# Graph-transformer layer with an LSTM: row stages in chunks of 256 rows, one ahead of the loop and four inside it

## The reference

```python
# layer 0, graph branch (agg: attention-weighted sums per node)
att = agg.reshape(n, C) @ Wo.T + bo
x = x + att
z = _layernorm(x, ln_ff_g, ln_ff_b)
h = jax.nn.silu(z @ W1.T + b1)
ff = h @ W2.T + b2
return x + ff
# layer 0, recurrent branch, on _layernorm(x), 1250 time steps
combined = jnp.concatenate((x_t, h_prev), axis=1)
f_t = jax.nn.sigmoid(combined @ W_f + b_f)
i_t = jax.nn.sigmoid(combined @ W_i + b_i)
c_tilde = jnp.tanh(combined @ W_c + b_c)
c_t = f_t * c_prev + i_t * c_tilde
o_t = jax.nn.sigmoid(combined @ W_o + b_o)
h_t = o_t * jnp.tanh(c_t)
```

## Time and profile before

| what | us |
|---|---|
| runs | 7319.33, 7336.98, 7514.56 |
| median | 7336.98 |
| the profiled execution | 7332.33 |
| its span, first to last instruction | 7330.6 |
| mean granted TensorE clock in it | 0.927 of full |

### The profile page before, as it was taken

How to read it: one execution, slowest core, us unless ns; L and a number is a source line. 1 busy time by engine, 2 the same in 40 slices (tenths; PEclk the granted TensorE clock), 3 DMA queues, 4 the chain that set the end, 5 groups by cost and what they waited for, 6 DMA issues and landing times. The chain is left out here.

```text
span 7330.6 us, 411790 instructions
## 1 busy us (share of the span) xinstructions
PE 5252.2 (72%) x180989; PEld 3541.9 (48%) x180989; DVE 3870.4 (53%) x22246; ACT 1844.6 (25%) x8790; POOL 875.2 (12%) x891
## 2 busy tenths in 40 slices
PE   1256354775977777777777777777777777877799
PEld 1122122442555555555555555555555555553445
DVE  6115355733466666666666666666666666573112
ACT  1001004820033333333333333333333333200011
POOL 0717563500000000000000000000000000350000
PEclk7677677987999999999999999999999999997899
DMA  2116465511000000000000000000000000230100
GB/s 71 40 70 200 138 175 100 159 37 46 0 0 0 0 0 0 0 0 0 0 0 0 0 0 0 0 0 0 0 0 0 0 0 0 86 80 23 46 0 15
DMA packets 116203, 235.83 MB, mean 32 GB/s; under 512 B 65390, under 2 KB 67054, under 8 KB 112251
## 3 DMA queue, kind: packets, MB, share of 16 engines
q0 software_dynamic: 56032, 162.48, 7.9%
q1 hardware_dynamic: 60058, 72.02, 3.2%
HBM read 219.99 MB, written 14.45 MB: 32 GB/s over the span
## 5 line engine op out<-in xcount | busy, mean ns | idle before, releaser
L1422 PE MATMUL l_bank<-l_w,l_hp 128*32 128x128 f16 x160000 | 2464.4, 219 | 998.7 <-DVE l_hp L1531 993.6
L1422 PEld LDWEIGHTS l_bank<-l_w,l_hp 128*32 128x32 f16 x160000 | 2246.3, 97 | 1633.0 <-DVE l_hp L1531 1627.4
L1495 DVE STREAM_TRANSPOSE l_turn<-l_bank 128x128 f32<-128x128 f32 x2500 | 794.5, 318 | 1180.0 <-PE l_bank L1422 1005.6
L1461 ACT ACTIVATE l_th<-l_z 128x8 f32<-128x8 f32 x2500 | 523.3, 209 | 2127.1 <-DVE l_z L1501 2127.1
L1443 PE MATMUL l_spare<-l_w 128*2 128x512 f16 x15000 | 1025.7, 379 | 0.0
L1674 POOL DMA_INDIRECT ga_rows<-r_table,dst_t x176 | 168.0, 955 | 4643.7 <-DMA r_table<-c_r 4516.4
L1466 ACT ACTIVATE l_tc<-l_th 128x2 f32<-128x2 f32 x2500 | 490.9, 196 | 464.3 <-DVE l_th L1518 464.3
L1507 DVE SCALAR_TENSOR_TENSOR l_terms<-l_th 128x4 f32<-128x4 f32 x2500 | 359.2, 144 | 256.1 <-ACT l_th L1461 256.1
L1525 DVE TENSOR_TENSOR l_hp<-l_go,l_tc 128x2 f16<-128x2 f32 x2500 | 422.0, 169 | 130.4
L1501 DVE TENSOR_REDUCE l_z<-l_turn 128x8 f32<-128x24 f32 x2500 | 447.2, 179 | 42.6
L1531 DVE TENSOR_TENSOR l_hp<-l_full,l_hp 128x2 f16<-128x2 f32 x2500 | 422.2, 169 | 43.2
(11 more groups left out here) (413 smaller groups left out, 4896.0 us busy)
## 6 DMA issues: line engine op xcount, KB each, us to landing
keys<-in_src_by_tile SPq DMA_DIRECT2D x7, 1344.0 KB
e_w<-in_e_W SPq DMA_DIRECT2D x2, 4096.0 KB
w<-in_g_W SPq DMA_DIRECT2D x2, 2048.0 KB, 10.4
l_wh<-in_l_Wh SPq DMA_DIRECT2D x1, 4096.0 KB
l_wx<-in_l_Wx SPq DMA_DIRECT2D x1, 4096.0 KB
e_w<-in_e_W SPq DMA_DIRECT2D x2, 2048.0 KB
sm_q_rows<-q_table,sorted_e POOLq DMA_INDIRECT x176
sm_k_rows<-k_table,sorted_e POOLq DMA_INDIRECT x176
```

The costliest lines, as they stand in the source:

```text
L1422: mm = pe.matmul(banks[par][q][32 * j:32 * j + 32, 0:128], hp[:, par, k, 30 - 30 * v:62 - 30 * v], w16[:, part, k, j, 256 * q + 128 * v:25 ...
L1461: act.activation(th[:, 2 * q:2 * q + 2, 1:], z[:, q, :].rearrange("p (j m) -> p j m", m=GATES), ACT.Tanh, scale=2.0 ** -Z_BITS).then_inc(s ...
L1495: dve.transpose(turn[:, par, q, :, 1:33], banks[par][q][:, 0:128].rearrange("p (m r) -> p m r", r=32)).then_inc(s_turned[q], 1)
```

## The change

The stages from the denominators to the input projection are no longer run over all rows. Rows are cut into five chunks of W = 256. The work on one chunk is a list of 101 numbered pieces, and each engine has at most one of its own per number:

| pieces | work | TensorE, per piece |
|---|---|---|
| 0 to 3 | transposes, copy on ScalarE | two transposes |
| 4 to 11 | output product, residual on VectorE | two matmuls of 256 columns |
| 12 to 24 | feed-forward LayerNorm | two matmuls in four pieces |
| 25 to 40 | first product; tanh form of silu on ScalarE | two matmuls |
| 41 to 56 | second product | two matmuls |
| 57 to 68 | LayerNorm for the recurrence | two matmuls in four pieces |
| 69 to 100 | input projection, written by ScalarE | two matmuls |

Chunk 0 runs ahead of the loop, all pieces one after another, with the packing of Wh and the remaining divisions between them. Chunks 1 to 4 run inside the loop: chunk c has its piece i at the end of step 256(c - 1) + i, on each engine behind that engine's own part of the step. These steps are written out (416 in all, with the few at chunk borders); the others stay in hardware loops, now five. A step in which TensorE has a piece issues four spare matmuls in place of twelve. The sigmoid becomes 0.5 (1 + tanh(x/2)), so ScalarE needs no table but that of tanh, except for the root: there it loads the table of the root and afterwards that of tanh again. `xp` holds two chunks instead of all rows and is scratch for the chunk being made. W2 and Wo share a buffer, and SyncE reloads them for each chunk. The maximum of Wh and its scales move into `scatter_and_tables`, with a 4 MB read of Wh ahead of the other weights there; Wh (again), Wo, W1 and the small columns load during `attend`; Wx loads into Wh's place after the packing.

The diff, cut to its core:

```diff
 def scatter_and_tables(...):
         def _(pool):
 ...
+            pool.wait_ge(topped, 1)
+            pool.partition_all_reduce(top[:, 1:2], top[:, 0:1], P, RMAX).then_inc(reduced, 1)
             pool.wait_ge(scattered, 16 * ET)
         def _(sp):
             for k in range(KC):
                 sp.dma_start(x[:, k, :], d["x"][:, k * NP:(k + 1) * NP]).then_inc(x_in, 16)
+            sp.dma_start(wh[:, :], d["l_Wh"]).then_inc(wh_in, 16)
             for dst, src in loads:
 ...
         def _(dve):
             for layer, (src, dst) in enumerate(((x, xn), (xn, z))):
+                if layer == 1:
+                    dve.wait_ge(wh_in, 16)
+                    g.link(dve, dve.tensor_reduce(top[:, 0:1], wh[:, :], AX.X, ALU.max, apply_absolute_value=True))
+                    dve.tensor_scalar(top[:, 0:1], top[:, 0:1], 2.0 ** -20, None, ALU.max).then_inc(topped, 1)
 def attend(...):
+        def _(sp):
+            for dst, src in loads:
+                sp.dma_start(dst, src).then_inc(loaded, 16)
+            sp.wait_ge(loaded, 16 * len(loads))
 ...
+W = 256
+CHUNKS = RT * P // W
+TURN, WO, LNF, FF1, FF2, LNL, XIN, STEPS = 0, 4, 12, 25, 41, 57, 69, 101
 ...
         def _(sp):
+            for c in range(CHUNKS):
+                wait_pe(sp, c, LNF - 1)
+                sp.dma_start(wo_w2, d["g_W2"]).then_inc(w2_in, 16)
+                if c == 0:
+                    sp.wait_ge(s_packed, M16)
+                    sp.dma_start(late[:, :], d["l_Wx"]).then_inc(wx_in, 16)
+                if c < CHUNKS - 1:
+                    wait_pe(sp, c, LNL - 1)
+                    sp.dma_start(wo_w2[:, 0:KC * C], d["g_Wo"]).then_inc(wo_in, 16)
 ...
         def _(pe):
+            def step(t, par, c=0, i=None):
 ...
-                for k in range(3):
+                busy = i is not None and on_pe(i)
+                for k in range(1 if busy else 3):
                     for j in range(4):
                         pe.matmul(spare[32 * j:32 * j + 2, 0:512], w16[:, 0, k, j, 0:2], w16[:, 0, k, j, :],
                                   start=True, stop=True)
-            with pe.Fori(0, N, 2) as t:
+                if busy:
+                    rows_step(c, i)
+            for i in range(STEPS):
+                if on_pe(i):
+                    rows_step(0, i)
+            pe.wait_ge(s_packed, M16)
+            for c in range(1, CHUNKS):
+                a = (c - 1) * W
+                for t in range(a - 2 if a else 0, a):
+                    step(t, t % 2)
+                for i in range(STEPS + 1):
+                    step(a + i, i % 2, c, i if i < STEPS else None)
+                with pe.Fori(a + STEPS + 1, a + W - 2, 2) as t:
+                    step(t, 0)
+                    step(t + 1, 1)
+            for t in range(a + W - 2, a + W):
+                step(t, t % 2)
+            with pe.Fori(a + W, N, 2) as t:
                 step(t, 0)
                 step(t + 1, 1)
         def _(act):
+                    elif j == 5:
+                        wait_dve(act, c, i - 1)
+                        act.activation(rstd, rstd, ACT.Sqrt).then_inc(row_act, 1)
+                        act.preload_act_table(ACT.Tanh)
 ...
+                elif i < FF2:
+                    m = (i - FF1) // 2
+                    wait_pe(act, c, i)
 ...
+                    act.activation(gate[:, m % 2, :], row_bank[m % 2][:, 0:W], ACT.Tanh, scale=0.5,
+                                   bias=b1_half[:, m:m + 1])
+                    act.activation(hid[:, m, :], row_bank[m % 2][:, 0:W], ACT.Identity, scale=0.5,
+                                   bias=b1_half[:, m:m + 1]).then_inc(row_act, 1)
 ...
+            for i in range(STEPS):
+                if on_act(i):
+                    rows_step(0, i)
+                if WO <= i < WO + M16:
+                    v, o, s = packing(*divmod(i - WO, GATES))
+                    act.activation(o[:, 0], v, ACT.Copy, scale=s).then_inc(s_high, 1)
         def _(dve):
+                    elif j < 10:
+                        quarter = slice((j - 6) * W // 4, (j - 5) * W // 4)
+                        if j == 6:
+                            wait_act(dve, c, i - 1)
+                        dve.reciprocal(rstd[:, quarter], rstd[:, quarter]).then_inc(row_dve, 1)
 ...
+            for i in range(STEPS):
+                if on_dve(i):
+                    rows_step(0, i)
+                if WO <= i < WO + M16:
+                    v, o, s = packing(*divmod(i - WO, GATES))
+                    dve.wait_ge(s_high, i - WO + 1)
+                    dve.scalar_tensor_tensor(o[:, 1], v, s, o[:, 0], ALU.mult, ALU.subtract).then_inc(s_packed, 1)
+                if FF2 + 4 <= i < FF2 + 4 + RT - 2:
+                    divide(i - FF2 - 2)
```

More of the change, by code:

```diff
@@ L33 @@
 EPS = 1e-5
+GATES = 4
+M16 = KC * GATES
+Z_BITS = 20
+SPREAD = 31
 class Ctx:
@@ L1209, in kernel_body @@
                           lambda dve: dve.tensor_copy(dst_t[:, :], by_tile[:, :, 2].bitcast(I32))])
[L1210 to L1292, removed]
@@ new lines, in on_dve, with up_to, rows_and_lstm @@
+def on_dve(i):
+    return (WO <= i < LNF and (i - WO) % 2 == 1 or i - LNF in (1, 2, 4, 6, 7, 8, 9, 10, 11)
+            or i - LNL in (1, 2, 4, 6, 7, 8, 9, 10, 11) or FF1 + 2 <= i <= FF2
+            and (i % 2 == 1 or i - FF1 in (3, 5, 7, 9)) or FF2 <= i < LNL and (i - FF2) % 4 == 3)
+def up_to(has, c, i):
+    return c * sum(has(j) for j in range(STEPS)) + sum(has(j) for j in range(i + 1))
+def rows_and_lstm(g, d, x, h, acc, wo_w2, w1, columns, late, spare_rows, spare_column, scale, h_scale):
@@ L1418, in rows @@
             def rows(par, q, k, first=False, signal=None):
-                for part in range(2):
+                for half in range(2):
                     for v in range(2):
@@ L1459, in step @@
+            def step(t, par, row, c=0, i=None):
                 for q in range(2):
@@ L1473, in _ @@
-            lay_input(0, 0)
-            with act.Fori(0, N, 2) as t:
-                step(t, 0)
-                step(t + 1, 1)
+                if i is not None and on_act(i):
+                    rows_step(c, i)
+            act.preload_act_table(ACT.Tanh)
+            for i in range(STEPS):
[4 more added lines that the diff above has]
+                    act.activation(o[:, 0], v, ACT.Copy, scale=s).then_inc(s_high, 1)
@@ new lines, in _ @@
+            wait_act(act, 0, STEPS - 1)
+            act.wait_ge(s_clean, 1)
+            lay_input(input_of(0), 0)
+            for c in range(1, CHUNKS):
+                a = (c - 1) * W
+                for t in range(a - 2 if a else 0, a):
+                    if t == a - 1:
+                        wait_act(act, c - 1, STEPS - 1)
+                    step(t, t % 2, input_of(t + 1))
+                for i in range(STEPS + 1):
+                    step(a + i, i % 2, input_of(a + i + 1), c, i if i < STEPS else None)
+                shift_in = (c - 1) % 2 * W - a
+                with act.Fori(a + STEPS + 1, a + W - 2, 2) as t:
+                    step(t, 0, bass.ds(t + (1 + shift_in), 1))
+                    step(t + 1, 1, bass.ds(t + (2 + shift_in), 1))
@@ L1478, in _ @@
+            wait_act(act, CHUNKS - 1, STEPS - 1)
+            for t in range(a + W - 2, a + W):
+                step(t, t % 2, input_of(t + 1))
+            shift_in = (CHUNKS - 1) % 2 * W - a - W
+            with act.Fori(a + W, N, 2) as t:
+                step(t, 0, bass.ds(t + (1 + shift_in), 1))
+                step(t + 1, 1, bass.ds(t + (2 + shift_in), 1))
         @block.vector
         def _(dve):
-            for par in range(2):
-                for q in range(2):
-                    dve.memset(banks[par][q][:, :], 0.0)
@@ L1548, in step @@
                 low(t, par, 1)
-            with dve.Fori(0, N, 2) as t:
+                if i is not None and on_dve(i):
+                    rows_step(c, i)
+            g.link(dve, dve.tensor_scalar(denom[:, 1, :, :], blocks[:, :, C:], 0.0, None, ALU.is_equal))
+            g.link(dve, dve.tensor_tensor(denom[:, 0, :, :], blocks[:, :, C:], denom[:, 1, :, :], ALU.add))
+            g.link(dve, dve.reciprocal(denom[:, 0, :, :], denom[:, 0, :, :]))
+            divide(0)
+            divide(1)
@@ new lines, in _ @@
+            for par in range(2):
+                for q in range(2):
+                    dve.memset(banks[par][q][:, :], 0.0)
+            for u in range(2):
+                g.link(dve, dve.tensor_copy(half_h[:, u:u + 1], h_scale[:, 0:1]))
+            g.link(dve, dve.memset(th[:, :, :], 0.0))
+            dve.memset(turn[:, :, :, :, :], 0.0).then_inc(s_clean, 1)
+            g.link(dve, dve.memset(hp[:, 1, :, :], 0.0))
+            dve.memset(hp[:, 0, 0:2, :], 0.0).then_inc(s_h[0], 1)
+            dve.memset(hp[:, 0, 2:4, :], 0.0).then_inc(s_h[1], 1)
@@ new lines, in _ @@
+            for c in range(1, CHUNKS):
+                a = (c - 1) * W
+                for t in range(a - 2 if a else 0, a):
+                    step(t, t % 2)
+                for i in range(STEPS + 1):
```

(7 more changed lines are left out.)

367 lines of the change are left out of this document (268 added, 99 removed).

## The result

The median is 7211.75 us (7190.51 to 7218.52, four runs) against 7335.96 us beside it: ratio 0.983, interval 0.980 to 0.986, 1.7% less where 4.8% was forecast, above the range's upper end of 7090. One of the four runs of the kernel before (7514.56 us) was a slower state of the chip and is not in the ratio. The profiled execution took 7218.5 us with a span of 7216.7.

What follows compares the result with a forecast made beforehand. A chain through TensorE, VectorE and ScalarE was taken to pace the recurrent loop, no engine full. 7330.6 - 379.4 - 1.5 + 1 + 8 + 14 + 12 = 6984.7 us of span, so 6986 measured; range 6945 to 7090.

Steps and rivals of the forecast that it cites:

- The part ahead of the loop: From the aggregation's last add to the first recurrent matmul: chunk 0 alone takes 102.4 us in place of 481.8, net -379.4.
- The roots: Inside the loop, ScalarE's root with two table loads does not fit its gap: 8 x 1.8 = 14 us more.
- +1 and +8: Work moved earlier: +1 us for Wh's reduction in the scatter stage, +8 us for 7.3 MB of loads in the aggregation.
- For the thin margins I add 0.03 us x 404 = 12: Inside the loop, allowance for pieces that only just fit the engines' gaps: 12 us over 404 steps with a piece.
- rival A: Written-out loop steps wait for TensorE instructions: at 4.1 us a packet, 416 steps add 580 us, giving 7566; chance 0.04.
- inside the loop: Sum for the 416 written-out steps: pieces fit the engines' gaps, adding only 14 us for roots and 12 for margins.
- free up to 2.9 us: In written-out loop steps, instruction fetching costs nothing while a packet comes within 2.9 us.
- break-even at 3.6: In written-out loop steps, a packet in 3.6 us, or 0.84 us more a step, would cancel the gain.
- 1.17: Instruction packets a written-out loop step needs, from about 275 instructions a step and about 235 a packet.
- the 235: Estimated instructions in each 16 KB packet of queue 8, from 5989 matmuls and as many loads outside the loop and 51 packets.
- an idle DMA: Inside the loop, reloads of Wo and W2 (12.6 MB) have 29 steps or 99 us each; no time was added.
- C: Back edges of the five loops fetch instructions at each turn: 312 us in one chunk loop, 1710 in all; chance 0.04.

Runs made afterwards that it cites:

- the ten runs below: The follow-up runs: variants of the changed kernel with loop pieces, TensorE loops, matmuls or spare matmuls altered; measured from 6548.1 to 7677.7 us.
- pe_out: Changed kernel without the row stages of chunks 1 to 4 and their loads; only TensorE's 416 steps written out, no pieces: 7225.5 us, ratio 0.984.

## Why the prediction was wrong

**Right.** The part ahead of the loop: 99.6 us for 102.4. First matmul at 1585.90 for "near 1590". The roots: TensorE's starts around one are 1658.65 and 1663.70, 5.05 us apart; the excess of 1.64 x 8 is 13 us for 14.

**Right in part by luck.** Scatter and aggregation: the last add comes 7.0 us later, for +1 and +8. The aggregation, from its first gather to its last add, took 308.5 us for 299.7, which is the +8; in the ten runs below it took 306.7 to 317.6. The +1 is not tested: up to the loop those ten have the code of the changed kernel, and yet the stage behind the scatter begins anywhere from 476.9 to 539.3 us in them (539.9 before, 531.8 in the changed kernel). The last add lies between 1434.8 and 1511.2 for the same reason.

**Too dear.** "For the thin margins I add 0.03 us x 404 = 12": in loops the pieces cost nothing that can be seen.

**The step that failed** is the dismissal of rival A, and with it the sum "inside the loop", which gave the instruction stream no term. It measured 266.4 - 13 = 253 us, 0.61 us a step (pe_out, with no piece and no root, has 263.0). The rest of the error is -12 -3 -2 -1, for the margins, chunk 0, scatter with aggregation, and the roots; that gives 235 where the span was missed by 232 us. A was described rightly, down to "queue 8 at some 500 packets"; its working failed in three ways.
- Its evidence against: "the loop's second step, read for the first time like any written-out code" at full speed. Two steps are two packets. The changed kernel's own first two written-out steps also took 3.41 and 3.47 us (1585.90, 1589.31, 1592.78), and the third 4.07. The first steps say nothing of the rate at which packets can be had. The two packets that queue 8 brought there before (at 1964.29 and 1968.05 us) are 3.76 us apart, as they are in the changed kernel (median 3.76 in its written-out steps), though the loop would have used up a packet in 3.1 us; the prediction did not use them.
- Its price was a point (4.1 us a packet from an unrelated landing time) with a chance of 0.04, and it was listed as a rival for "slower" only. Between "free up to 2.9 us" and "break-even at 3.6" lay a stretch in which the kernel is still faster, but by less, and the truth is there: 1.08 packets (448 in 416 steps) of 3.7 us are 4.0 us a step. Nothing in the trace excluded that stretch, and the range should have held it, up to the point where 0.84 x 416 us eat up the whole gain of 350.
- The packets per step were 1.08, not 1.17, since a packet is 256 instructions; the 235 came from dividing other stages' matmuls by packets. With that, free ends at 3.17 us and the break-even is 3.95.

**A smaller term was also put at nothing**: the reloads of W2 and Wo, with "an idle DMA". Queue 8 was not idle. In the changed kernel's written-out steps 433 of the 439 distances between two packets are under 5 us; the other six, 5.7 to 6.9 us, all lie at a reload. Around the first one, a 2 MB reload that takes 8.4 us, the packets come at 1631.42 and 1638.36 us:

```profile
1632.53 0.33 SPq L1380 DMA_DIRECT2D wo_w<-in_g_W  x1
1636.49 1.13 PE L1487 MATMUL l_bank<-l_w,l_hp 128*32 128x128 f16 x67 [0.15 <-DVE l_hp L1730]
1640.86 1.05 PE L1487 MATMUL l_bank<-l_w,l_hp 128*32 128x128 f16 x61 [3.24 <-issue]
```

The six are 16 us beyond the median in all, a part of the 253. pe_out, which has no reloads, has no distance over 5 us among 450. That the reload holds the packets up is argued from this; no run took the reloads alone out of the changed kernel.

The Trainium skill (Runtime: NRT & Kernel Launch, Instruction fetch mechanics) has the sequencer load the next 16 KiB page while it executes the current one, mostly hidden. The packet size agrees: the cut moves by just what a step has beyond 256 instructions. "Mostly hidden" held with half the matmuls, at 5.5 us a packet, and failed where 3.2 were wanted.

**C** did not occur: plain steps stayed at 3.41. The mechanism behind it exists, but over a size: bodies of some 1680 instructions and more were fetched again on each turn. The same section of the Trainium skill says that a branch to a target outside the two-page window stalls; here a body of 1540 instructions, six pages, turned back without one, so for TensorE the window was wider than two pages.

## What to carry to other kernels

Unrolling is a cost of its own where an engine issues faster than its code arrives: count the instructions of a step on the densest engine, divide by the rate (here 70 a us on TensorE, 256 in about 3.7 us), and compare with the step's time; at 128 small matmuls in 3.4 us the step was just over. Keep the dense engine in a loop whose body fits (1540 instructions did) and unroll only the others, staging by DMA what would need an address that changes. And where a rival's mechanism is credible but its price unknown, give it its whole stretch of prices in the range, the part with a smaller gain too.

## What the hardware showed that was not expected

In 47 cuts of the changed kernel between 1640 and 1930 us, from the records of the queue's packets in the trace: TensorE resumes 1.41 us after a packet has landed (1.29 to 1.53 in the middle eight tenths), the next packet starts 1.13 us after that (1.05 to 1.59), and it takes 1.10 us. Together 3.64 us, near the median distance of two packets there, 3.73. It looks as if one packet is asked for only when the one before has been entered; that is read from the order of events, and no run took it apart.

Dropping the spare matmuls saved 84 us of the loop while the clock stayed at 0.97 to 0.98: filler meant for the clock is itself instructions to fetch.

Taking out half of a step's matmuls shortened it by only 0.36 us (3.41 to 3.05), since only the matmuls ahead of the first bank's transpose lie in the chain. From a step's first matmul to the transpose of the first bank it is 1.06 us where it was 1.35, and from there to the next step's first matmul 1.99 for 2.06.
